# The norms' sums of squares moved from VectorE to ScalarE, and other opening work of VectorE moved or dropped, in an eight-block model on one core

## The reference, cut to what matters

```python
h = jnp.einsum('blv,dv->bld', x, Win) + bin
def body(h, p):
    y = jax.nn.silu(layernorm(h, l1w, l1b))
    y = sconv(y, pr + 1j * pi, lr + 1j * li)     # a decaying sum along the tokens
    h = h + y * scl
    y = layernorm(h, l2w, l2b)
    y = jax.nn.silu(jnp.einsum('bld,fd->blf', y, w1) + b1_)
    y = jnp.einsum('blf,df->bld', y, w2) + b2_
    return (h + y, None)
h, _ = jax.lax.scan(body, h, xs)                 # four layers
h = layernorm(h, lnl_w, lnl_b)
return jnp.einsum('bld,vd->blv', h, Wout) + bout
```

## Time and profile before

| | |
|---|---|
| median of 3 runs | 2315.28 us (2312.95 to 2316.45) |
| the profiled execution | 2311.02 us, its span 2309.3 us |
| PE busy | 2193.8 us, 95% of the span |
| DVE busy | 1434.1 us, 62% |
| ACT busy | 1200.4 us, 52% |
| POOL busy | 503.4 us, 22% |

### The profile page before, as it was taken

How to read it: one execution, slowest core, us unless ns; L and a number is a source line. 1 busy time by engine, 2 the same in 40 slices (tenths; PEclk the granted TensorE clock), 3 DMA queues, 4 the chain that set the end, 5 groups by cost and what they waited for, 6 DMA issues and landing times.

```text
span 2309.3 us, 35366 instructions
## 1 busy us (share of the span) xinstructions
PE 2193.8 (95%) x12528; PEld 1165.2 (50%) x12528; DVE 1434.1 (62%) x2909; ACT 1200.4 (52%) x2205; POOL 503.4 (22%) x610
## 2 busy tenths in 40 slices
PE   5689898999999999999999999999999999999998
PEld 5465544555455554555555555454534444444443
DVE  7876888868677685787878787878723222212212
ACT  5346688747566575666667666788751111011010
POOL 3423323313223122232323232223210000000000
PEclk8799899999999999999999999999999999999999
DMA  5003144314122141322323233333231000000000
GB/s 185 1 1 91 55 124 138 107 41 140 46 78 87 44 139 41 118 87 87 120 79 100 80 116 111 113 96 107 84 103 32 9 9 1 18 0 5 14 0 18
DMA packets 135774, 163.22 MB, mean 71 GB/s; under 512 B 42272, under 2 KB 97696, under 8 KB 135328
## 3 DMA queue, kind: packets, MB, share of 16 engines
q1 hardware_dynamic: 135600, 160.97, 22.7%
HBM read 94.19 MB, written 53.35 MB: 64 GB/s over the span
## 4 chain that ended last, share of the span: by engine, by line
PE 83%; DVE 6%; DMA 3%; ACT 2%; issue 2%; SPq 1%; POOL 0%; POOLq 0%; ACTq 0%; DVEq 0%
PE ps L1548 16%; PE ps L1446 9%; PE ps L1476 8%; PE ps L1559 8%; PE ps L1431 8%; PE ps L1455 7%; PE ps L1501 5%; PE ps L1401 3%; PE ps L1406 3%; PE ps L1510 2%; PE ps L1533 2%; PE ps L1319 2%; PE ps L1486 2%; DVE peaks L2165 2%; PE ps L1412 2%
## 5 line engine op out<-in xcount | busy, mean ns | idle before, releaser
L2165 DVE TENSOR_REDUCE peaks<-ps 128x4 f32<-128x512 f32 x960 | 625.3, 681 | 220.7 <-PE ps L1401 116.0
L1744 ACT ACTIVATE big<-ps 128x512 f32<-128x512 f32 x960 | 547.0, 602 | 246.1 <-PE ps L1431 240.7
L1969 POOL TENSOR_SCALAR_AFFINE_SELECT big<-big 128x512 f32<-128x512 f32 x384 | 259.2, 688 | 891.9 <-ACT big L1744 890.4
L1548 PE MATMUL ps<-xt,big 128*128 128x512 f32 x896 | 393.4, 597 | 2.9 <-issue 2.9
L1431 PE MATMUL ps<-big 99*128 99x512 bf16 (+3 forms) x1536 | 340.1, 302 | 11.6 <-DMA big<-scr_shift 6.2
L1548 PEld LDWEIGHTS ps<-xt,big 128*128 128x128 f32 x896 | 169.9, 191 | 211.0 <-issue 209.7
L1853 ACT ACTIVATE t<-ps 128x512 f32<-128x512 f32 x56 | 33.5, 599 | 452.3 <-PE ps L1548 452.3
L1476 PE MATMUL ps<-xt,big 128*128 128x512 f32 x480 | 247.5, 607 | 1.3 <-ACT xt L1759 1.1
L1446 PE MATMUL ps<-big,vs 128*32 128x512 f32 (+3 forms) x3072 | 241.1, 441 | 6.0 <-POOL big L1969 4.2
L1732 ACT ACTIVATE ps<-cbf 128x512 f32<-128x512 bf16 x384 | 232.3, 605 | 21.2 <-DVE peaks L2165 15.0
L2221 DVE SCALAR_TENSOR_TENSOR t<-rest,t 128x512 f32<-128x512 f32 x56 | 38.7, 691 | 283.7 <-PE ps L1548 282.6
(11 more groups left out here) (234 smaller groups left out, 2886.3 us busy)
## 6 DMA issues: line engine op xcount, KB each, us to landing
big<-scr_q SPq DMA_DIRECT2D x96, 384.0 KB, 3.9
scr_q<-big SPq DMA_DIRECT2D x48, 384.0 KB, 2.7
scr_q<-big SPq DMA_DIRECT2D x48, 256.0 KB, 3.0
recb<-scr_sums SPq DMA_DIRECT2D x96, 128.0 KB
big<-scr_k SPq DMA_DIRECT2D x48, 192.0 KB, 3.3
big<-in_ffn_gu SPq DMA_DIRECT2D x14, 512.0 KB, 5.1
scr_q<-big SPq DMA_DIRECT2D x48, 128.0 KB, 2.9
ctxt<-ots SPq DMA_DIRECT2D x192, 32.0 KB, 2.0
```

The costliest lines, as they stand in the source:

```text
L1548: mm = pe.matmul(bank_of(kind, n, m), wgu[:, m // 2, c, way, m % 2 * P:(m % 2 + 1) * P], xt[:, c, :], start=(c == 0), stop=(c == DC - 1))
L1744: act.activation(probs[:, place(g, i) * S:(place(g, i) + 1) * S], bank_of("exp", g, i), ACT.Exp, scale=1.0 / 16 if attn_of(n) == 1 else 0. ...
L1969: pool.affine_select(block_, block_, [[0, GQ], [1, P]], ALU.is_ge, zero, base=0, channel_multiplier=-1).then_inc(made["cut"], 1)
L2165: dve.tensor_reduce(to, blocks, AX.X, ALU.max, negate=True).then_inc(made["negmax"], 1)
```

## The change

The sums of squares are made by ScalarE: four activations of 64 columns for each norm instead of one of 256, each with an output that adds up its columns, with the 1/64 in the scale. GpSimd adds epsilon (from a small constant tile) ahead of the power. `hs` is gone from VectorE. The second norm of a lane-layer writes 64 columns for each tile instead of two copies of them (`hn1`). The output bias is row 64 of `wout`, met by a row of ones that the last `ut` makes, so `last_bias` is gone from GpSimd. The fills of `begin` are GpSimd's now, at the start of its program; the ones of `kt` are one fill of all of `kt` (`ones`), which the keys' first transfer waits for. The 4-bit codes and scales are loaded ahead of the rows of sequences 2 and 3. The decode's third piece gets room of its own (`dq3`), so that it no longer waits for the tables. The assumed durations change with these.

```diff
     if kind == "hln":
-        return [("ACT", "hq", k, 480), ("DVE", "hs", k, 620), ("POOL", "hr", k, 1150), ("DVE", "hx", k, 750)]
+        return [("ACT", "hq", k, 1560), ("POOL", "hr", k, 1450), ("DVE", "hx", k, 430 if k[2] else 750)]
...
-            load_rows(2)
-            load_rows(3)
             load("fp4", (codes, ins["fp4_codes"]))
...
-            load("out", (wout, ins["ssm_wout"]), (lnl[:], ins["ssm_lnl"]),
-                 (bias_of["last"], ins["ssm_bout"].broadcast_to((P, D))))
+            load_rows(2)
+            load_rows(3)
+            load("out", (wout[0:64], ins["ssm_wout"][0:64]), (wout[64:65], ins["ssm_bout"]),
+                 (wout[65:P], ins["ssm_wout"][65:P]), (lnl[0:64], ins["ssm_lnl"][0:64]))
...
             def keys(p):
...
+                if p == 0:
+                    sp.wait_ge(made["ones"], counted("ones"))
...
-                act.activation(hq[q], ps[:, H_BANKS[q], 0:256], ACT.Square).then_inc(made["hq"], 1)
+                for j in range(TJ):
+                    last = act.activation(hq[q][:, 64 * j:64 * (j + 1)], h[q][:, j], ACT.Square, scale=0.125,
+                                          accum_out=hsm[:, q, 0, j:j + 1])
+                last.then_inc(made["hq"], 1)
...
-            def last_bias(b, j):
-                pool.wait_ge(weights["out"], 48)
-                pool.wait_ge(made["inx_full"], counted("inx_full", b, DC - 1))
-                pool.tensor_tensor(x_rows(b, j), x_rows(b, j), bias_of["last"], ALU.add).then_inc(made["resl"], 1)
-
             def h_rstd(l, q, k):
-                pool.wait_ge(made["hs"], counted("hs", l, q, k))
+                pool.wait_ge(made["hq"], counted("hq", l, q, k))
+                pool.tensor_tensor(hsm[:, q, 1], hsm[:, q, 0], small[:], ALU.add).then_inc(pool_links, 1)
+                pool_linked[0] += 1
+                pool.wait_ge(pool_links, pool_linked[0])
                 pool.tensor_tensor(hsm[:, q, 2], hsm[:, q, 1], half[:], ALU.pow).then_inc(made["hr"], 1)
...
+            pool.memset(small[:], EPS)
             pool.memset(half[:], -0.5).then_inc(tables, 1)
-            pool.wait_ge(tables, 1)
+            pool.memset(peaks[:], 3.0e38).then_inc(tables, 1)
+            pool.memset(shp[:], 0.0).then_inc(tables, 1)
+            pool.memset(vs[:], 0.0).then_inc(clearing, 1)
+            pool.wait_ge(tables, 3)
...
+                elif kind == "ones":
+                    pool.wait_ge(made["tab_d"], counted("tab_d", 9))
+                    pool.memset(kt, 1.0).then_inc(made["ones"], 1)
...
-            def h_squares(l, q, k):
-
-                dve.wait_ge(made["hq"], counted("hq", l, q, k))
-                then(dve.tensor_reduce(hsm[:, q, 0], hq[q].rearrange("p (j d) -> p j d", d=64), AX.X, ALU.add))
-                dve.tensor_scalar(hsm[:, q, 1], hsm[:, q, 0], 1.0 / 64, EPS, ALU.mult, ALU.add).then_inc(made["hs"], 1)
-
             def norm_h(l, q, k):
                 dve.wait_ge(made["hr"], counted("hr", l, q, k))
+                if k:
+                    dve.tensor_tensor(hn1[q], h[q], hsm[:, q, 2].unsqueeze(2).broadcast_to((P, TJ, 64)), ALU.mult
+                                      ).then_inc(made["hx"], 1)
+                    return
...
             def begin():
 
-                dve.memset(peaks[:], 3.0e38)
-                dve.memset(shp[:], 0.0)
-                dve.memset(vs[:], 0.0).then_inc(clearing, 1)
-                dve.wait_ge(clearing, 1)
-                dve.memset(vs[:].rearrange("p k j h d -> p (k j h) d")[:, :, HD:HD + 1], 1.0).then_inc(clearing, 1)
-                dve.wait_ge(made["decode"], counted("decode", DC - 1))
-                dve.memset(kt[KROWS:SROWS], 1.0).then_inc(ready, 1)
+                dve.wait_ge(tables, 3)
                 dve.wait_ge(constants, 16)
                 dve.tensor_copy(cbf[:], t1[:, 0:3 * P]).then_inc(constants, 1)
```

More of the change, by code:

```diff
@@ L153, in four_bit @@
 def four_bit(b):
-    items = [("resl", b, j) for j in range(TJ)]
+    items = []
     for j in range(TJ):
@@ L293, in pieces @@
     if kind in ("sel", "begin", "half_bias", "centre_in", "centre_out"):
-        return [("DVE", kind, (), {"sel": 1000, "begin": 3000, "half_bias": 250, "centre_in": 1100, "centre_out": 2800}[kind])]
+        return [("DVE", kind, (), {"sel": 1000, "begin": 600, "half_bias": 250, "centre_in": 1100, "centre_out": 2800}[kind])]
     if kind == "decode":
+        ones = [("POOL", "ones", (), 2700)] if k[0] == DC - 1 else []
         return [("ACT", "sign", k, 1150), ("POOL", "signed", k, 1260), ("DVE", "mag", k, 750), ("ACT", "steps", k, 1150),
-                ("DVE", "decode", k, 2200)]
+                ("DVE", "decode", k, 2200)] + ones
     if kind == "y":
@@ L394, in order_of @@
     if name in ("sel", "centre_out"):
-        return [("x_in", (2,))]
+        return [("lw_in", ())]
+    if name == "ones":
+        return [("tab_d", (9,))]
     if name == "begin":
-        return [("decode", (DC - 1,))]
+        return [("out_in", ())]
     if name == "half_bias":
@@ L572, in order_of @@
     if name == "keys":
-        return [("cw", (n // NPAIR, CH - 1))] + ([("exp_full", (2 * n - 5, UNITS - 1))] if n >= 3 else [])
+        return [("cw", (n // NPAIR, CH - 1)), ("ones", ())] + ([("exp_full", (2 * n - 5, UNITS - 1))] if n >= 3 else [])
     if name == "queries":
@@ L743, in needs @@
                     return out
-                if tag == "l":
-                    out.append(("resl", (n, j)))
-                elif tag == "f" or (tag == "d" and attn_of(n) == 1):
+                if tag == "f" or (tag == "d" and attn_of(n) == 1):
                     out.append(("resid", (tag, n)))
@@ L968, in program @@
         half = sb("half", [P, TJ], F32)
+        small = sb("small", [P, TJ], F32)
         ident = sb("ident", [P, P], F32)
@@ L983, in program @@
         bias_ys = sb("bias_ys", [P, 2, D], F32)
-        bias_of = {"last": bias_ys[:, 0, :], "attn1": bias_ys[:, 1, :], "ffn1": bias_ys[:, 0, :],
+        bias_of = {"attn1": bias_ys[:, 1, :], "ffn1": bias_ys[:, 0, :],
                    "experts": bias_ys[:, 1, :]}
@@ L1039, in program @@
         scl4 = big1[:, 4096:6144]
-        dq3 = big1[:, 6144:8192]
+        dq3 = [big1[:, at:at + D] for at in (8704, 9216, 14336, 14848)]
         codes = big1[:, 10240:12288].bitcast(I32)
@@ L1059, in program @@
         hn = [f.rearrange("p (j k d) -> p j k d", k=2, d=64) for f in hf]
+        hn1 = [f[:, 256:512].rearrange("p (j d) -> p j d", d=64) for f in hf]
         hq = [f[:, 0:256] for f in hf]
@@ L1369, in project_out @@
                 pe.wait_ge(made["ut"], counted("ut", NL, b, 0))
-                pe.wait_ge(weights["out"], 48)
+                pe.wait_ge(weights["out"], 64)
                 pe.matmul(bank_for("last", b, j), u[b][:, j * P:(j + 1) * P], wout, start=True, stop=True
@@ L1687, in code_steps @@
                 act.activation(codes.bitcast(F32)[:, cols], dq2[:, cols], ACT.Relu, bias=steps_at[:, 1:2])
-                act.activation(dq3[:, cols], dq2[:, cols], ACT.Relu, bias=steps_at[:, 2:3], scale=2.0
+                act.activation(dq3[quarter], dq2[:, cols], ACT.Relu, bias=steps_at[:, 2:3], scale=2.0
                                ).then_inc(made["steps"], 1)
@@ L1694, in turned_h @@
                 if l == NL:
-                    act.wait_ge(weights["out"], 48)
+                    act.wait_ge(weights["out"], 64)
                     act.activation(u[q], bank, ACT.Identity, bias=lnl[:, 1:2], scale=lnl[:, 0:1]
@@ L1703, in turned_h @@
                 else:
-                    act.activation(u[q], bank, ACT.Identity, bias=lw[:, l, 3:4], scale=lw[:, l, 2:3]
+                    act.activation(u[q][0:64], bank[0:64], ACT.Identity, bias=lw[0:64, l, 3:4], scale=lw[0:64, l, 2:3]
                                    ).then_inc(made["ut"], 1)
@@ L1987, in _ @@
                     flow_bias(*k)
-                elif kind == "resl":
-                    last_bias(*k)
                 elif kind == "lo":
@@ L2351, in _ @@
             w8 = (P, TJ, 8)
-            small = [sm[:, 9, TJ * k:TJ * (k + 1)] for k in range(6)]
+            smalls = [sm[:, 9, TJ * k:TJ * (k + 1)] for k in range(6)]
             def s8(k):
@@ L2360, in gating_logits @@
                 logits = ag[:, :, P:136]
-                then(dve.tensor_reduce(small[0], logits, AX.X, ALU.max))
-                dve.tensor_tensor(s8(0), logits, small[0].unsqueeze(2).broadcast_to(w8), ALU.subtract
+                then(dve.tensor_reduce(smalls[0], logits, AX.X, ALU.max))
+                dve.tensor_tensor(s8(0), logits, smalls[0].unsqueeze(2).broadcast_to(w8), ALU.subtract
                                   ).then_inc(made["logits"], 1)
@@ L2374, in gating_weights @@
                 then(last)
-                dve.tensor_copy(sm[:, 8, 0:1], small[2][:, 0:1])
+                dve.tensor_copy(sm[:, 8, 0:1], smalls[2][:, 0:1])
                 for j in range(TJ):
```

51 lines of the change are left out of this document (22 added, 29 removed).

## The result

The changed kernel takes 2300.99 us (median of 10 runs, 2293.11 to 2313.58), beside 2313.96 us for the kernel before in the same session: a ratio of 0.9955, 95% interval 0.994 to 0.9971. By the 0.2% that the prediction takes as what can be told from no change, it is faster. A second session gave 2302.6 and 0.995 (0.9932 to 0.9969). The profiled execution took 2293.11 us and was the fastest of its ten, so its 17.9 us less span than before is more than the 9 to 13 us of the medians.

The account below looks back on a forecast made before the run. PE bounds the kernel behind 350 us, VectorE is late in the opening; first `exp` at 158.4 + 62.3 + 36.5 = 257 instead of 267.3, -11 us in all, so 2311.0 becomes 2300, median 2304, range 2289 to 2316.

Parts of the forecast that it names:

- the 257 of the forecast: Start of the first `exp`: 158.4 + 62.3 + 36.5 = 257 us, instead of 267.3.
- The decode: Opening, VectorE: without GpSimd's additions 12 instructions cost about 0.7 us instead of 1.3 to 1.64, saving 8 to 11 us.
- Lane 0's `f` stays at 59, lane 1's at 68.4: Opening: lane 0's first `f` gains nothing; lane 1's starts at 68.4 instead of 84.2 us, a lead of 15.8.
- c = 1.5 (1.0 to 3.0): ScalarE's price in us of one norm's four squares with added outputs, with lower and upper bounds.
- The lane-layer at 7.0 us: Lane 1's `f` to first `last`: 12.8 lane-layers at an unchanged 7.0 us make 90 us, `last` at 158.
- rival C: The whole gain: c = 1.0 saves 4 us in the opening, lane-layers at 6.4 us; -23 us, median 2292; chance 0.18.
- `last` to `max` unchanged, `max` to `exp` 7 us shorter: Behind the first `last`: 62.3 us stay to `max`; then two fewer lane-layers cut VectorE's stretch to 36.5 us.
- rival A: Given back by order: `last` to `exp` stays 105.8 us, first `exp` at 264.2, -3 us, median 2312; chance 0.16.
- Whatever shortens the opening moves all of this forward: Behind 350 us, where PE is busy 1915 of 1959 us: an opening's lead carries through to the end.
- Rival B: ScalarE becomes the bound: zero gain at about c = 2.45, at 3.0 +21 us, median 2336; chance 0.09.
- Rival D: Decode still contends with GpSimd's `signed_scales`, VectorE stays late by half: -5 us, in the forecast's range; no chance given.
- The edits at nothing: Fills (large one 1.8 to 5 us), `ones` (2.6 to 7.6), mask cast, load order, `last_bias`: about no effect on time.

Follow-up runs that it names:

- e1: Kernel before with only the last product's bias moved into the weights and GpSimd's 16 opening additions removed; 2306.7 us, ratio 0.9979.
- e6: Kernel after, same order, with each of GpSimd's 48 remaining bias additions split into four pieces of 128 columns; 2288.9 us, ratio 0.9898.
- e3: Kernel after, same order, with each norm's four squares on ScalarE made a second time into unused columns; 2316.0 us, ratio 1.0015.
- e7: Kernel before with both squares on ScalarE and bias in the weights, but its old fills, load order and decode room; 2302.7 us, ratio 0.9955.
- e11: Kernel after with split additions, and rows of x of lanes 2 and 3 loaded ahead of the fp4 codes again; 2289.7 us, ratio 0.9898.
- e9: Kernel before, same order, with all 64 of GpSimd's bias additions split into four pieces of 128 columns; 2301.1 us, ratio 0.994.

## Why the prediction held, step by step

The direction and the number held (2304 forecast, 2301 and 2302.6 measured), but two steps were off by more than the difference, in opposite directions. That they nearly cancelled is luck: the first `exp` came 9 to 12 us ahead of the 257 of the forecast (248.4 and 245.1), and 4 to 11 us of lead were lost behind it, where the forecast lost none.

*The decode* at 0.69 us, and the `hx` of lanes 2 and 3 ahead of the last quarter: right. e1 shows that VectorE was what lane 1 waited for: without the additions its `f` came 10 us earlier behind nearly the same list of VectorE. One reading was too simple: of the four instructions behind the 1636 ns of the earlier trace rows, the first (45.67 us) ran beside `signed_scales`, not beside the additions. Its quarter is fast in after (0.69 us, from 37.9 to 40.0) because the new order has GpSimd idle there until 40.2, not because the additions are missing.

*Lane 0's `f` stays at 59, lane 1's at 68.4:* right in effect, 60.9 and 67.8. Its make-up was not: `f` took 1.98 us, not 3.56, as the clock was up, and the squares 0.8. Both profiles of after agree to 0.1 us here; with the low clock elsewhere in the opening e6 has 68.0 and 74.9 in the same order, so a term taken at a low clock was a matter of luck. (ACT's sum as written gives 59.0, not 58.9.)

*c = 1.5 (1.0 to 3.0):* too high, 0.8 us, and outside the bounds. The lower bound had the reads overlap by 0.1 us on each side; the trace shows the next activation starting 0.1 us behind the read's start, whatever the read's own 0.2 us. The estimate of 1.3 us from the Trainium skill ("ScalarE: Activation LUTs", What ACT_TABLE_LOAD costs) was too high for the same reason: it laid the reads end to end.

*The lane-layer at 7.0 us:* mis-sized with c. e3 gives 7.16 at c = 1.6, close to what was said for 1.5; at 0.8 it is 6.4 (52 instructions of `f`, 13.0 lane-layers, stood in that window, where the forecast had 12.8). That put the first `last` at 149.7 instead of 158. In this rival C ("the whole gain", c = 1.0, 6.4 us) described the opening better than the forecast did.

*`last` to `max` unchanged, `max` to `exp` 7 us shorter:* 61.0 against 62.3, and 9.1 shorter (34.4 us; 34.6 in the second profile). Right, and rival A (105.8 us kept) fell: it is 95.4.

*"Whatever shortens the opening moves all of this forward":* this step failed. A lead of 22.2 us at the first `exp` was 18.3 at the end of `exp` in the first profile, and 18.9 became 7.8 in the second. The coincidences of VectorE's short instructions with GpSimd's remaining 48 additions took it, in waits of 1.9 to 3.8 us and the lower clock behind several of them. I had named that contention for the decode and read it nowhere else. e6 took it away and gained 12 us or more.

*Rival B* was nearer than its 0.09: it put the turning point at c = 2.45 (its own terms, 8 x (c - 1.5) and 12.8 x (2c - 4.4) against 11, give 2.36), and e3 shows no gain left at 1.6. Had c been what I took it for, the time would have been about 2316, not 2304. *Rival D*, the decode beside `signed_scales`: one of 12 instructions in after, 1.75 us, and three of 12 in before and in e1. *The edits at nothing* were that together (e7), and the load order alone (e11); the sizes were not, as the large fill of GpSimd took 1.8 us and `ones` 2.7, not 5 and 7.6.

## What to carry to other kernels

A gain in an opening reaches the end only if what follows keeps its pace: compare the lead at three or four later events, not only at the end. Where small VectorE instructions are suddenly as long as a GpSimd instruction beside them, cut the GpSimd instruction into short pieces before moving work between engines; here that edit of a few lines was worth as much as the whole change that was studied, and 1.0% with it. Two edits that relieve the same queue are to be tried together as well as alone: one of these was worth -0.2%, the other +0.2%, both -0.45%. Where an order is planned anew with each edit, as here, the new order is part of what is measured.

## What the runs showed of the hardware

An activation of 64 columns with an added output takes 0.22 us and its read 0.2, but a pair comes every 0.20 us, where 512 columns needed 0.75. TensorE's granted clock fell behind single waits of 2.9 to 3.8 us in a stretch that was otherwise full, and behind one of 1.87 it did so at 858.8 us of after (0.50 from 859 to 862 us) but not at 1358.3 (1.00 for the next 3 us); with the additions split it stayed at 1.00 for 1221 us, in which no wait of PE was longer than 1.3 until one of 1.95 at the very end. And short pieces help only some instructions: beside a back-to-back row of GpSimd pieces an addition of 512 columns took 0.83 us, but the cast of 384 columns took 7.53, until the row ended (e9, one occurrence).
